# 36 routed blocks with paired small last blocks, eight row homes, and weight products of the table on GpSimd

## What is computed

```python
logits = xf @ gate_w.T                                  # 2048 x 8
topk_logits, topk_idx = jax.lax.top_k(logits, 2)
topk_w = softmax(topk_logits)
comb = zeros((N, E)).at[arange(N)[:, None], topk_idx].add(topk_w)
for e in range(8):
    g, u = xf @ wg[e].T, xf @ wu[e].T                   # 256 -> 384 each
    out = out + comb[:, e:e + 1] * (silu(g) * u @ w_down[e].T)
shared = silu(xf @ sg_gate.T) * (xf @ sg_up.T) @ sg_down.T
x = x + tanh(g_ffn) * (shared + out)
```

## Time and profile before

| | us |
|---|---|
| median of 3 runs (lowest, highest) | 510.13 (507.63, 510.97) |
| the profiled execution | 509.94 |
| its span, first to last instruction | 508.2 |

### The profile page before, as it was taken

How to read it: one execution, slowest core, us unless ns; L and a number is a source line. 1 busy time by engine, 2 the same in 40 slices (tenths; PEclk the granted TensorE clock), 3 DMA queues, 4 the chain that set the end, 5 groups by cost and what they waited for, 6 DMA issues and landing times.

```text
span 508.2 us, 7908 instructions
## 1 busy us (share of the span) xinstructions
PE 489.0 (96%) x2876; PEld 305.4 (60%) x2876; DVE 303.9 (60%) x551; ACT 263.9 (52%) x418; POOL 176.3 (35%) x196
## 2 busy tenths in 40 slices
PE   8999999999999999999789999999999999999992
PEld 7665432333333333334265466699999999999992
DVE  3765789999999999975574794233333333333321
ACT  1666277777777777776615102134444444444430
POOL 4600187882211111210000003006666666656643
PEclk9999999999999999999979999999999999999997
DMA  7633418858542664211031012023434433433432
GB/s 246 222 103 103 126 64 229 214 151 206 170 126 65 173 203 123 65 32 55 0 108 59 2 41 82 2 94 51 66 61 72 65 62 64 62 65 63 62 43 32
DMA packets 36886, 48.71 MB, mean 96 GB/s; under 512 B 6288, under 2 KB 29968, under 8 KB 36848
## 3 DMA queue, kind: packets, MB, share of 16 engines
q1 hardware_dynamic: 21536, 26.16, 18.3%
q0 software_dynamic: 7488, 10.23, 12.9%
q10 hardware_dynamic: 7824, 11.81, 7.2%
HBM read 30.55 MB, written 14.29 MB: 88 GB/s over the span
## 4 chain that ended last, share of the span: by engine, by line
PE 94%; DVE 2%; ACT 1%; issue 1%; POOLq 0%; POOL 0%; DVEq 0%
PE ps L1123 77%; PE ps L1209 12%; PE ps L1457 2%; PE ps L1129 1%; DVE neg_max L824 1%; PE ps L1342 1%; ACT ctx_region L681 1%; PE ps L1139 1%; PE ps L1201 0%; PE ps L1351 0%; POOLq L105 0%; DVE o_sb L865 0%; ACT xnT L708 0%; ACT xnT L636 0%; ACT unit_region L627 0%
## 5 line engine op out<-in xcount | busy, mean ns | idle before, releaser
L681 ACT ACTIVATE ctx_region<-ps 128x512 f32<-128x512 f32 x256 | 140.7, 594 | 47.0 <-PE ps L1123 47.0
L824 DVE TENSOR_REDUCE neg_max<-ps 128x2 f32<-128x1024 f32 x128 | 150.9, 1208 | 21.3 <-PE ps L1123 19.4
L1123 PE MATMUL ps<-unit_region 96*128 96x512 bf16 (+1 forms) x512 | 128.4, 380 | 0.9 <-ACT ctx_region L681 0.7
L1123 PE MATMUL ps<-unit_region,ctx_region 128*128 128x128 f32 (+1 forms) x968 | 114.0, 274 | 0.0
L1123 PEld LDWEIGHTS ps<-unit_region,ctx_region 128*128 128x128 f32 (+1 forms) x968 | 110.6, 189 | 0.7 <-issue 0.3
L1123 PEld LDWEIGHTS ps<-unit_region 96*128 96x128 bf16 (+1 forms) x512 | 45.0, 97 | 101.0 <-ACT ctx_region L681 45.2
L573 POOL DMA_INDIRECT out<-unit_region x39 | 61.7, 1583 | 55.2 <-DMA out<-unit_region 48.4
L546 POOL DMA_INDIRECT unit_region<-x_rows,unit_region x39 | 38.6, 990 | 117.8 <-DVE unit_region L1066 80.7
L1123 PE MATMUL ps<-dn_region,unit_region 128*128 (+1 forms) x330 | 78.4, 379 | 0.0
L741 ACT COPY ctx_region<-up_region 128x1536 f32 x39 | 57.3, 1472 | 34.7 <-PE ps L1123 34.6
L1087 DVE TENSOR_TENSOR unit_region<-unit_region,ps 128x384 f32<-128x384 f32 x38 | 21.0, 553 | 81.3 <-ACT unit_region L758 74.9
(11 more groups left out here) (152 smaller groups left out, 395.4 us busy)
## 6 DMA issues: line engine op xcount, KB each, us to landing
up_region<-in_w_upT ACTq DMA_DIRECT2D x9, 768.0 KB, 4.4
qk_parts<-up_region SPq DMA_DIRECT2D x24, 192.0 KB, 3.1
unit_region<-qk_parts SPq DMA_DIRECT2D x24, 192.0 KB, 4.2
dn_region<-in_w_downT ACTq DMA_DIRECT2D x9, 384.0 KB, 5.2
unit_region<-up_region SPq DMA_DIRECT2D x48, 64.0 KB, 2.6
unit_region<-qk_parts SPq DMA_DIRECT2D x24, 128.0 KB, 4.3
ctx_region<-in_ctxT SPq DMA_DIRECT2D x4, 512.0 KB, 11.1
x_rows<-rows SPq DMA_DIRECT2D x4, 512.0 KB, 3.6
```

Of the source, the lines that this page charges most:

```text
L681: nc.scalar.activation(probs[:, k % 8, :], bank(SCORE_HOME[u, k]), ACT.Exp).then_inc(exp_done, 1)
L824: nc.vector.tensor_reduce(neg_max[:, s, 2 * p:2 * p + 2], bank(2 * (p % 2), 2), AX.X, ALU.max, negate=True).then_inc(max_done, 1)
L1123: return nc.tensor.matmul(o_, w, m, start=start, stop=stop)
```

## The change

The routed blocks are worked in 36 slots instead of 39. An expert whose last block holds at most 64 rows may have that block put into one half (64 rows) of a paired slot; slots 5, 13 and 21 are paired and take up to six such halves. Where fewer experts have a small last block, the halves are partly unused; an assertion covers all counts. The adds to the output stay 39: a paired slot is added twice, once for each half. A paired slot's up products take x as the stationary operand, 64 columns for each half, and 384 weight columns moving: the first half reads the expert's weights at a run-time address, the second a copy that ScalarE makes (`half_up`, `half_dn`, in the place of `xnT`). The hidden rows then have to be turned (three turns in bank 5, inside the next up products) and copied by VectorE before the down products, which are made in two 64-column halves too. Rows of x have eight homes instead of four (in the place of `rows`), results four instead of two. GpSimd writes twenty runs of two order tables at the start. The step from counts to slots on VectorE grows. The three weight products of the table move from VectorE to GpSimd, and `make_table` waits for them. Behind the row marks six steps are added that name the experts of the halves (the first two are shown).

```diff
-MAX_BLOCKS = (TOPK * N + E * (P - 1)) // P
+ADDS = (TOPK * N + E * (P - 1)) // P
+PAIR_SLOTS = 3
+SLOTS = ADDS - PAIR_SLOTS
+HALF_P = P // 2
+HALVES = 2 * PAIR_SLOTS
+PAIR_STEP = 9
+HALF_SHIFT = PAIR_SLOTS * P + HALF_P
+PAIR_ADDS = tuple(5 + PAIR_STEP * q for q in range(PAIR_SLOTS))
...
+ADD_OF = []
+FILL = []
+for j in range(SLOTS):
+    if len(ADD_OF) in PAIR_ADDS:
+        FILL.append(SLOTS - 1 - PAIR_ADDS.index(len(ADD_OF)))
+        ADD_OF += [(j, 0), (j, 1)]
+    else:
+        FILL.append(j - sum(i >= SLOTS - PAIR_SLOTS for i in FILL))
+        ADD_OF.append((j, None))
+assert PAIR_ADDS[0] + PAIR_STEP * PAIR_SLOTS <= ADDS
...
-ROW_HOMES = 4
+ROW_HOMES = 8
...
+        half_up = xnT[:, 0, 0:DC * FFN].rearrange("p (c f) -> p c f", c=DC)
+        half_dn = xnT[:, 1, 0:FC * D].rearrange("p (f n) -> p f n", f=FC)
...
+            fill_order(iota_b, [FILL[j] + (PAIR_SLOTS if half else 0) for j, half in ADD_OF])
+            fill_order(iota_a, [FILL[j] for j, _ in ADD_OF])
...
+            pool.wait_ge(marks_set, 1)
+            for c in range(3):
+                nc.gpsimd.tensor_tensor(block_values[:, :, WEIGHT + c, :], block_marks[:, :, :],
+                                        weight_parts[:, c, :].unsqueeze(2).to_broadcast([P, PAIRS, ADDS]), ALU.mult).then_inc(weights_set, 1)
+                pool.wait_ge(weights_set, c + 1)
             pool.wait_ge(rows_out, 16 * B)
             pool.wait_ge(table_set, 1)
...
+                if half != 1 and j + ROW_HOMES < SLOTS:
                     gather(j + ROW_HOMES)
...
+            def copy_half(q):
+                a = PAIR_ADDS[q] + 1
+                load_experts(a)
+                if q:
+                    act.wait_ge(by_ps, PAIR_AT[q - 1] + 1)
+                nc.scalar.copy(half_up[:, :, :].rearrange("p c f -> p (c f)"),
+                               w_up[:, bass.ds(chosen_expert[a], 1), :, :].rearrange("p a c f -> p (a c f)"))
+                nc.scalar.copy(half_dn[:, :, :].rearrange("p f n -> p (f n)"),
+                               w_dn[:, bass.ds(chosen_expert.pop(a), 1), :, :].rearrange("p a f n -> p (a f n)")
+                               ).then_inc(half_copied, 1)
+            def copy_up(n):
...
-            step(nc.vector.tensor_scalar(count_i[:, :], count[:, :], float(P - 1), None, ALU.add))
-            step(nc.vector.tensor_scalar(blocks_i[:, :], count_i[:, :], 7, None, ALU.logical_shift_right))
-            step(nc.vector.tensor_copy(blocks[:, :], blocks_i[:, :]))
+            nc.vector.tensor_scalar(count_i[:, :], count[:, :], float(P - 1), None, ALU.add)
+            step(nc.vector.tensor_scalar(halves_i[:, :], count[:, :], float(HALF_P - 1), None, ALU.add))
+            nc.vector.tensor_scalar(blocks_i[:, :], count_i[:, :], 7, None, ALU.logical_shift_right)
+            step(nc.vector.tensor_scalar(halves_i[:, :], halves_i[:, :], 6, None, ALU.logical_shift_right))
+            nc.vector.tensor_copy(blocks[:, :], blocks_i[:, :])
+            step(nc.vector.tensor_copy(halves[:, :], halves_i[:, :]))
+            step(nc.vector.scalar_tensor_tensor(small[:, :], blocks[:, :], 2.0, halves[:, :], ALU.mult, ALU.subtract))
+            step(nc.vector.tensor_tensor_scan(smalls[:, :], ones_bf[:, 0:E], small[:, :], 0.0, ALU.mult, ALU.add))
+            step(nc.vector.scalar_tensor_tensor(moved[:, :], smalls[:, :], float(HALVES), small[:, :], ALU.is_le, ALU.mult))
+            step(nc.vector.tensor_tensor(blocks[:, :], blocks[:, :], moved[:, :], ALU.subtract))
+            nc.vector.tensor_tensor(key[:, :], moved[:, :], smalls[:, :], ALU.mult)
+            nc.vector.tensor_scalar(limit[:, :], blocks[:, :], float(P), None, ALU.mult)
             step(nc.vector.tensor_tensor_scan(ends[:, :], ones_bf[:, 0:E], blocks[:, :], 0.0, ALU.mult, ALU.add))
-            step(nc.vector.tensor_tensor(base[:, :], ends[:, :], blocks[:, :], ALU.subtract))
-            step(nc.vector.scalar_tensor_tensor(rank[:, :, :], base[:, :].unsqueeze(1).to_broadcast([P, NT, E]),
-                                                float(P), rank[:, :, :], ALU.mult, ALU.add))
+            nc.vector.tensor_tensor(base[:, :], ends[:, :], blocks[:, :], ALU.subtract)
+            nc.vector.tensor_tensor(in_half[:, :, :], rank[:, :, :], limit[:, :].unsqueeze(1).to_broadcast([P, NT, E]),
+                                    ALU.is_ge)
+            nc.vector.tensor_scalar(beyond[:, :], ends[:, :], float(-P), float((SLOTS - 1) * P - HALF_SHIFT), ALU.mult, ALU.add)
+            nc.vector.tensor_scalar(shift_a[:, :], key[:, :], 3.0, float(-2 * HALF_SHIFT - P), ALU.is_ge, ALU.mult)
+            step(nc.vector.tensor_scalar(shift_b[:, :], key[:, :], 5.0, float(-2 * HALF_SHIFT - P), ALU.is_ge, ALU.mult))
+            nc.vector.scalar_tensor_tensor(rank[:, :, :], base[:, :].unsqueeze(1).to_broadcast([P, NT, E]),
+                                           float(P), rank[:, :, :], ALU.mult, ALU.add)
+            nc.vector.scalar_tensor_tensor(beyond[:, :], key[:, :], float(HALF_SHIFT), beyond[:, :], ALU.mult, ALU.add)
+            step(nc.vector.tensor_tensor(shift_a[:, :], shift_a[:, :], shift_b[:, :], ALU.add))
+            step(nc.vector.tensor_tensor(beyond[:, :], beyond[:, :], shift_a[:, :], ALU.add))
+            step(nc.vector.tensor_tensor(in_half[:, :, :], in_half[:, :, :],
+                                         beyond[:, :].unsqueeze(1).to_broadcast([P, NT, E]), ALU.mult))
+            step(nc.vector.tensor_tensor(rank[:, :, :], rank[:, :, :], in_half[:, :, :], ALU.add))
+            shared_hidden(1, range(1))
...
+            dve.wait_ge(order_set, order_steps[0])
+            nc.vector.tensor_tensor(
                 block_marks[:, :, :], block_of[:, :, :].rearrange("p k t -> p (k t)").unsqueeze(2).to_broadcast(
-                    [P, PAIRS, MAX_BLOCKS]), iota_b[:, :].unsqueeze(1).to_broadcast([P, PAIRS, MAX_BLOCKS]), ALU.is_equal))
-            dve.wait_ge(const_step, 9)
+                    [P, PAIRS, ADDS]), iota_b[:, :].unsqueeze(1).to_broadcast([P, PAIRS, ADDS]), ALU.is_equal
+                ).then_inc(marks_set, 1)
+            dve.wait_ge(marks_set, 1)
             nc.vector.tensor_scalar(block_values[:, :, PLACE, :], block_marks[:, :, :], place[:, 0:1], None, ALU.mult)
             for k in range(TOPK):
                 pairs = slice(k * NT, (k + 1) * NT)
                 nc.vector.tensor_tensor(block_values[:, pairs, TILE, :], block_marks[:, pairs, :],
-                                        iota_b[:, 0:NT].unsqueeze(2).to_broadcast([P, NT, MAX_BLOCKS]), ALU.mult)
-            shared_hidden(1, range(1))
-            for c in range(3):
-                nc.vector.tensor_tensor(block_values[:, :, WEIGHT + c, :], block_marks[:, :, :],
-                                        weight_parts[:, c, :].unsqueeze(2).to_broadcast([P, PAIRS, MAX_BLOCKS]), ALU.mult)
+                                        iota_t[:, :].unsqueeze(2).to_broadcast([P, NT, ADDS]), ALU.mult)
             shared_hidden(1, range(1, 2))
+            shared_hidden(1, range(2, FC))
             dve.wait_ge(lag_done, 2)
...
-                if i == 0:
-                    shared_hidden(1, range(2, FC))
-                elif i == 1:
+                if i == 1:
                     shared_added(0)
...
+            step(nc.vector.tensor_tensor(hits[:, :, :], key[:, :].unsqueeze(1).to_broadcast([P, HALVES, E]),
+                                         iota_e[:, 1:1 + HALVES].unsqueeze(2).to_broadcast([P, HALVES, E]), ALU.is_equal))
+            step(nc.vector.tensor_reduce(hit[:, :], hits[:, :, :], AX.X, ALU.add))
...
+            def copy_hT(q, s):
+                dve.wait_ge(bhT_ps, q + 1)
+                nc.vector.tensor_copy(blk_h[:, s, :], bank(5)[:, 0:HALF]).then_inc(bhT_sb, 1)
...
+                    if i == 0:
+                        pe.wait_ge(weights_set, 3)
...
+            def up_pair(j, s):
                 pe.wait_ge(bxT_sb, j + 1)
-                pe.wait_ge(up_copied, j + 1)
+                pe.wait_ge(half_copied, PAIR_AT.index(j) + 1)
+                pe.wait_ge(bhid, j - 1)
+                for g in range(2):
+                    cols = slice(g * HALF, (g + 1) * HALF)
+                    for c in range(DC):
+                        nc.tensor.matmul(
+                            bank(2 * s + g)[0:HALF_P, 0:HALF], blk_xT[:, s, c, 0:HALF_P],
+                            w_up[:, bass.ds(expert[ADDS_OF[j][0]], 1), c, cols].rearrange("p a f -> p (a f)"),
+                            start=c == 0, stop=c == DC - 1, skip_group_check=True)
+                        last = nc.tensor.matmul(
+                            bank(2 * s + g)[HALF_P:P, 0:HALF], blk_xT[:, s, c, HALF_P:P], half_up[:, c, cols],
+                            start=c == 0, stop=c == DC - 1, skip_group_check=True)
+                    last.then_inc(bup_ps, 1)
+            def turn_hidden(j, s):
+                q = PAIR_AT.index(j)
+                pe.wait_ge(bhid, j + 1)
+                if q:
+                    pe.wait_ge(bhT_sb, q)
```

(54 more changed lines are left out.)

230 lines of the change are left out of this document (150 added, 80 removed).

## The result

The changed kernel takes 502.58 us (median of 4 runs, 501.53 to 503.27), the kernel before 509.35 us over all its runs by then: ratio 0.987, interval 0.985 to 0.990. The forecast was 506.7 and "within 1%"; the time lies inside its range of 499.5 to 510.5, but 4.1 us under the point, and the gain of 1.3% is clear of the noise and more than "within 1%".

What follows compares the result with a forecast made beforehand. TensorE was taken to bound the kernel. Blocks -12.6, pairs +2.4, weight products +5.5 and clock +1.5 sum to -3.2 us, from 509.94 to 506.7, within 1%; range 499.5 to 510.5.

Steps and rivals of the forecast that it cites:

- Three blocks: Block loop: three blocks fewer at 4.20 us each on TensorE, 12.6 us less.
- A paired block: Block loop: a paired slot's up, down and hidden-row turns cost 0.8 us more than a plain block, +2.4 for three.
- rival 3: Paired slots: column halves run one after the other, +4.2 us a pair instead of +0.8, 517 us; chance 0.05.
- rival 4: Paired slots: three blocks go but another wait sets in at the pairs, 2 us each, 512.7 us; chance 0.06.
- The adds, the homes, the constants, the half copies: Block loop and kernel start: extra queueing, twenty short iotas and ScalarE's weight copies are all covered and cost nothing.
- VectorE's chain: Before the table: more small VectorE steps between ranks and one-hot product, +2.9 us, plus 0.6 for a shared product moved ahead.
- The weight products: Table stretch: three products on GpSimd collide with VectorE's two-input SBUF products, so TensorE waits; +5.5 us, ends 0 and 6.7.
- in turns: Table stretch: only one of GpSimd and VectorE runs at a time, TensorE standing 2.9 us, then about 2.3 more: +5.2.
- The clock: Table stretch: TensorE's waits may drop its granted clock to 0.50; half the price taken, +1.5 us, ends 0 and 3.
- case with contention: The forecast case: GpSimd and VectorE hold each other before the table, 504.1 to 510.6 us; chance 0.70.
- case without contention: Table stretch: no contention that matters, GpSimd's weight products end by 302.7, 499.7 us; chance 0.19.
- The new profile's signs: Paired up about 2.8 us, loop about 10 shorter, slowed GpSimd or VectorE products, TensorE wait over 2, perhaps clock 0.5.

Runs made afterwards that it cites:

- e4_plain_slots: Changed kernel with the three paired slots worked as plain blocks, their second half with the first half's weights; 500.08 us.
- e1_write_only: Changed kernel with GpSimd's three weight products replaced by six memsets of the same tiles, TensorE waiting for the sixth; 498.34 us.
- e6_six_products: Changed kernel with GpSimd making the third weight product four times instead of once, TensorE waiting for the last; 509.82 us.
- v1_late_table: Changed kernel with TensorE making the table one shared up product later, after (2, 2) instead of (2, 1); 500.33 us.
- v2_early_shared: Changed kernel with the table one shared up product later, VectorE's shared products (1, 1), (1, 2) right behind the place product, shared sum before the row marks; 498.03 us.
- the control: Changed kernel with GpSimd testing the bounds of the values it loads for the waits of its adds; 502.26 us.

## Why the prediction was right or wrong

**Three blocks, -12.6.** Right: 12.59.

**A paired block, +0.8 each.** Right: 0.87. The parts: up with its changes of tile 2.9 forecast and 2.93 from the rows above (360.16 - 357.12 less 0.22 for the turns, plus 0.1 at the next start), turns 0.33, down 1.6 against 1.45 and 0.14 around it (0.09 ahead, 0.05 behind). Reading the price of a tile change from the group in the earlier trace rows carried over from four tiles to two. The halves abreast (rival 3) and the hidden waits (rival 4) are settled by the same rows and by `e4_plain_slots`.

**The adds, the homes, the constants, the half copies, nothing.** Right: TensorE is busy through the whole loop. The copies of the half weights were just covered, as worked out: ScalarE had 0.24 us to spare before the next silu.

**VectorE's chain.** +3.5 until the marks; measured 6.77 - 3.53 = 3.24 us (291.42 and 289.19 against the counts at 284.65 and 285.66). An unwaited small step is 0.08, not 0.1.

**The weight products, +5.5: this step failed in its size, by 2.1.** The mechanism was the one forecast: a VectorE product with two inputs in SBUF stands while GpSimd reads there, the first shared product comes late, TensorE waits before (2, 1) and before the table. Measured 3.4, in two waits of 1.4 and 1.6. Where the 5.2 of "in turns" was too much: from the end of the marks it has the third GpSimd product end 9.8 us later and the row marks 15.7. Measured are 8.3 and 14.1. The order of the turns and the full exclusion were right; the price of one GpSimd product was not. I had charged 2.6 us for each behind the VectorE instruction, scaled by elements from a row with an fp32 input; measured are 2.12 for each, three times 0.5 too much. The remainder of the 5.2, 0.3, is the shorter chain, and 0.3 more is that I took 5.5 instead of the 5.2.

One reading was right for the wrong reason: I counted the place product among those "of just that kind", two inputs in SBUF. It has one, yet GpSimd's product and copy were held until it ended (2.12 and 1.11 us after it, as behind the others).

The rule of the Trainium skill ("SBUF — State Buffer", "Who interferes with whom") was the right side to take: the runs now show both directions, and that writing alone does not hold a two-input product (`e1_write_only`). That VectorE's place product was held by a memset, and held GpSimd in turn, fits the same section, which lets instructions in a two-port mode contend with any GpSimd instruction; no run here shows the mode itself. "For the whole instruction" agrees too: GpSimd's products took 2.53, 2.71 and 3.13 us behind VectorE instructions of 0.55, 0.80 and 1.21 (the last in `e6_six_products`), and always ended 2.12 to 2.13 after them.

**The clock, +1.5: this step failed.** It was 0. I took half the price of a fall without a reason for the half: the earlier trace rows showed idle that did lower the clock, and no row showed idle that did not. The runs show waits of up to 2.2 us that leave it. The waits came out in two pieces of 1.2 and 1.4, shorter than the 2.9 and 2.3 I had, so the error in the size of the contention probably made this one too; no run had waits of 2.9 and 2.3 in this place. Its price was also too high: in `e6_six_products` the fall cost 1.3 us, since most of the slow time passed while TensorE waited.

**The sum.** -12.6 + 2.6 + 3.4 + 0 = -6.6, and the times differ by 509.35 - 502.58 = 6.8. I had -3.2: 2.1 too much for the weight products, 1.5 for the clock, 0.2 too little for the pairs. The point also started from the profiled execution, 509.94, which lies 0.6 over the median of 509.35.

That the time lies inside the range is luck. My case with contention reached from 504.1 to 510.6, and 502.58 lies under it; the range holds it only because it also took in the case without contention, and that mechanism did not happen. The new profile's signs came true for the paired products (2.73 us), the loop (10 us shorter) and the tile products (2.87), but no wait was over 2 us and no clock fell. The chances put 0.57 on "within 1%", because contention was believed, priced above its own "in turns", and given a clock fall on top; the lower bounds of the same case, -5.8, were the better estimate.

## What to carry to other kernels

Work moved from VectorE to GpSimd was free here only beside VectorE instructions that take one operand from PSUM; beside products with two inputs in SBUF it gave back more than it took, 5.0 us for 4.2. Price such a meeting as turns: each engine's instruction starts its work when the other's has ended. Where both engines must work, order VectorE's queue so that its PSUM work falls into GpSimd's instructions, and let TensorE take other work ahead of what they produce: `v1_late_table` won 1.9 us with the second of these and `v2_early_shared` 3.4 with both, without an instruction less. A second penalty that hangs on the length of a wait, as the clock's did here, takes over every error in that length: price it only once the wait itself is bounded.

## What the runs showed of the hardware that was not expected

- Where the turns go: with both queues full, one VectorE product and one GpSimd instruction ran in turn. A GpSimd product (bf16, two inputs, 128x1248) ended 2.12 to 2.13 us after the VectorE instruction before it, in all 24 cases of seven kernels, whether that was the place product, a tile product or a row mark; a tile product of 0.80 us that met a whole GpSimd product took 2.87 or 2.88.
- In `e1_write_only` a memset on GpSimd (1.17 us) held the place product (bf16, one SBUF input, 0.55 us alone) to 1.62 us, and the next memset, which began beside the place product, took 1.39. Memsets left two-input products of 0.80 us alone.
- GpSimd copies (1.25 us alone) and VectorE two-input products hold each other: 1.85 for 0.80, and 1.71 to 2.27 for 1.25.
- Two 64-column tiles run abreast with different moving operands, one of them read at a run-time address: 0.32 us a pair of 384-column fp32 passes.
- After a wait the granted clock can stay low although work has begun: in `e6_six_products` it fell 3.4 us into the wait and was low for 6.8 us, of which TensorE worked 2.7; in the kernel before it was low for 6.8 with 5.9 of work, and at the same place in the control for 3.4.
